# Single-row fetches by two DMA queues in a graph network on one Trainium2 core: byte offsets, loads of sixteen, higher rates and a third buffer

## The chip, the cores and the metric

The kernel runs on one core of a Trainium2 chip. The core has TensorE (PE, matrix products), VectorE (DVE), ScalarE (ACT), GpSimd (POOL) and SyncE (SP); each has its own instruction queue and works in the order of that queue, and the five meet at semaphores. DMAs are issued by SP, ACT and POOL and move data between DRAM and SBUF (128 partitions); PSUM holds the products. The metric is the device time of one execution in microseconds, smaller is better.

## The reference

The inputs are a graph of 12,500 nodes with 128 float32 features each and 212,500 edges, sorted by their target `dst`, with an `edge_weight` and a type from 0 to 7. Three layers follow each other (the file calls them layers 0, 1 and 2):

```python
edge_in = x[src] * edge_weight[:, None]                       # layer 0
msg = relu(edge_in @ W_msg + b_msg)
x1 = layernorm(x + relu(segment_sum(msg, dst) @ W_out + b_out))
xt = einsum('nd,rde->rne', h, W)                              # layers 1 and 2,
h = relu(segment_sum(xt[edge_type, src], dst) + h @ SW + b)   # from h = x1
out = layernorm(x1 + h)
```

Each layer gathers one row of 128 floats for every edge from a table in DRAM and adds the rows up by target. The tables are `msg_table` (12,500 rows, x times W_msg) and, for layers 1 and 2, `rel_table0` and `rel_table1` with one row for each node and type (100,352 rows).

## The kernel before

**Groups, tiles, steps.** The edges are cut into groups of eight tiles of 128 edges, 208 groups in layer 0 and 197 in each of layers 1 and 2. Two groups (16 tiles) make a step, so a layer has some 104 or 98 steps. In each step `fused_edges` handles two groups, and then `node_step` takes one block of 128 nodes, some steps behind the edges, through the layer's end (product, norm, next table). All five engines run through the same steps from lists written out by `fused_loop`; nothing is a loop on the chip.

**A group.** POOL gathers its tiles into `rows` (`static_gather`, L705, one indirect DMA for 128 rows), in a ring of eight groups: before it refills a slot it waits until PE has used it. DVE builds the one-hot matrices (L824) and in layer 0 scales every tile by its edge weights (L846); ACT applies relu in layer 0 (L673) or only passes the word on (L678); PE multiplies each tile with its one-hot matrix into PSUM (L872); DVE adds the result to `agg` (L859).

**The fetched tiles.** In some groups the eighth tile doesn't come from POOL. The class `Fetch` has it fetched row by row, by SP (`by_sync`, even groups) or by ACT (`by_act`, odd groups). `starts` and `rates` say from which step of each layer on, and how many rows a step: SP 24, 32 and 32, ACT 0, 24 and 24. So SP completes a tile in 5 1/3 steps in layer 0 and in 4 in the others, 17, 23 and 23 tiles; ACT makes 0, 17 and 17; in all 97 tiles, 12,416 rows. `Fetch.eight` does eight rows: it loads eight row numbers from the list `ids` in SBUF to registers (L801), and for each row computes the byte address in a register and starts a DMA of 512 bytes (L807). A tile is used two steps after its last row; it lies in one of `FETCHES` = 2 buffers of its queue, so that the first of its rows waits for the use of the tile before the last one (L795). The lists are made by DVE: for layer 0 a copy in `dve_layout`, for the others two instructions in `dve_trim`.

**Order on the queues.** SP's step is: the node work's DMAs (L1213 loads x, L1220 stores the table, L1226 stores the normed block), then its fetches. In layer 0 `sync_trim` puts more between them: for each of the two groups of a step a value load and a DMA to `kind_line` (L1584, L1586), with eight fetches behind each, then the DMA to `kind_of` (L1594), for which DVE waits before it picks each node's own row (L1140, L1147), and the last eight fetches. ACT's step is: the activations of the first group, eights number 0 and 2, those of the second group, eight number 1, then its node work, with the copy of the table from PSUM to SBUF (L1051) that DVE's second product (L1147) waits for. In layer 0 ACT fetches nothing.

Of the kernel before, what the change touches and what calls it, by code (L numbers as in the profile page):

```python
# [36 lines left out]
FETCHES = 2  # L37
EIGHT = 8
MOST = 80
# [60 lines left out]
def build(nc, x, src, dst, edge_type, edge_weight, W_msg, b_msg, W_out, b_out,  # L100
# [27 lines left out]
    with ctx:  # L128
# [6 lines left out]
        def ring_sems(name, n):  # L135
# [74 lines left out]
        extra = {"SP": spare_float[:, 2 * P:4 * P].rearrange("p (k d) -> p k d", k=2),  # L210
                 "ACT": spare_int[:, 4 * P:6 * P].bitcast(F32).rearrange("p (k d) -> p k d", k=2)}
# [160 lines left out]
        def dve_layout(sems, chunks, sorted_edges):  # L372
# [8 lines left out]
            for c in range(chunks):  # L381
# [8 lines left out]
                if not sorted_edges:  # L390
                    nc.vector.tensor_copy(ids[0][0:ROWS, c, :], e_src[:, GROUP - P:GROUP])
# [357 lines left out]
        class Fetch:  # L749


            def __init__(self, name, starts, rates, q):
                self.name = name
                self.starts = starts
                self.rates = rates
                self.groups = []
                self.base = []
# [16 lines left out]
            def tile(self, m):  # L774
                return extra[self.name][:, m % FETCHES, :]

            def wait(self, eng, m):

                eng.wait_ge(s_fetched[self.name][m % FETCHES], 16 * P * (m // FETCHES + 1))

            def eight(self, eng, layer, step, k):
# [7 lines left out]
                m, g = self.base[layer] + i, self.groups[layer][i]  # L789
                c, p = divmod(g, SIDE if layer else ROWS)  # L790
                if e == 0:
                    tables_ready(eng, layer)
                if part == 0:
                    if m >= FETCHES:
                        eng.wait_ge(edge_main.prod, self.uses[m - FETCHES] + 1)  # L795
                    if layer:
                        eng.wait_ge(s_stage, STAGES * c + PACKED)
                    else:
                        eng.wait_ge(lay.flag, 1)
                table = rel_tables[layer - 1] if layer else msg_table  # L800
                _, at = nc.values_load_multi_w_load_instructions(  # L801
                    ids[1 if layer else 0][p:p + 1, c, part * EIGHT:(part + 1) * EIGHT],
                    engines=[eng.engine], min_val=0, max_val=(NP * R if layer else N) - 1,
                    skip_runtime_bounds_check_because="the DMA checks its address")
                for j in range(EIGHT):
                    row = part * EIGHT + j
                    eng.dma_start(self.tile(m)[row:row + 1, :], table[bass.ds(at[j], 1), :]  # L807
                                  ).then_inc(s_fetched[self.name][m % FETCHES], 16)

        by_sync = Fetch("SP", (9, 1, 1), (24, 32, 32), 0)  # L810
        by_act = Fetch("ACT", (0, 1, 1), (0, 24, 24), 1)
# [623 lines left out]
        def dve_trim(step):  # L1435
# [27 lines left out]
            for c, beat in trim_beats(step):  # L1463
# [48 lines left out]
                else:  # L1512
                    closer(beat - BUILD_PACK - 1, 0)
                    if beat == BEATS - 1:
                        linked(v.tensor_scalar(held_int[0:r, 0:P], word[:, GROUP - P:GROUP],
                                               P.bit_length() - 1, None,
                                               ALU.logical_shift_right))
                        linked(v.tensor_scalar(ids[1][0:r, c, :], held_int[0:r, 0:P], -1.0, 0.0,
                                               ALU.add, ALU.max))
# [49 lines left out]
        def sync_trim(eng, step):  # L1569
# [27 lines left out]
            by_sync.eight(eng, 0, step, 2)  # L1597

        def fused_edges(eng, layer, step):
# [4 lines left out]
            for q in range(PAIR):  # L1604
# [22 lines left out]
                elif eng is nc.scalar:  # L1627
# [5 lines left out]
                    for k in range(q, by_act.rates[layer] // EIGHT, PAIR):  # L1633
# [204 lines left out]
```

## Time and profile before

| | |
|---|---|
| median of 3 runs | 8,691.48 us (8,671.66 to 8,698.19) |
| the profiled execution's own time | 8,760.86 us |
| its span | 8,759.1 us, 83,654 instructions |
| granted TensorE clock | 0.61 of full speed in the mean |
| PE busy | 2,867.2 us (33%) |
| weight loads (PEld) | 2,251.3 us (26%) |
| DVE busy | 2,703.9 us (31%) |
| ACT busy | 614.4 us (7%) |
| POOL busy | 4,471.7 us (51%) |
| DMA | 54 GB/s in the mean, 471 MB |
| rows fetched by SP | 2,176 from `msg_table`, 5,888 from the others |
| rows fetched by ACT | 4,352 |

The profile is of one execution; its times are a little over the median of the runs. Busy times leave out instructions that only handle registers, semaphores and branches, and those that issue DMAs; SP does nothing else, so it has no line there, and its queue (SPq) is to be read from the timeline, the chain and the views by line. A line such as L807 is that of the kernel's file. Layer 0 lasts from about 150 to 3,075 us, layer 1 from 3,137 to 5,855, layer 2 from 5,890 to the end.

### The profile page before, as it was taken

How to read it: one execution, taken by the hardware profiler on the slowest of the kernel's cores; microseconds unless marked ns; L12 is line 12 of the kernel's file. 1: busy time of each engine (PE TensorE's matmuls, PEld its weight loads, DVE VectorE, ACT ScalarE, POOL GpSimd, SP SyncE). 2: the span in 40 equal slices, each digit the busy share in tenths (PEclk: the TensorE clock that was granted, in tenths of full speed). 3: DMA queues.
4: the chain of work that ended last, by engine and by line, in shares of the span. 5: the costliest groups of instructions: out<-in, count | busy, mean ns of one | idle time of the engine just before them, and what ended most of it. 6: DMA issues, size and time to landing. Idle time of an engine off the chain costs nothing.

```text
span 8759.1 us, 83654 instructions
## 1 busy us (share of the span) xinstructions
PE 2867.2 (33%) x11892; PEld 2251.3 (26%) x11892; DVE 2703.9 (31%) x5898; ACT 614.4 (7%) x1351; POOL 4471.7 (51%) x4738
## 2 busy tenths in 40 slices
PE   5233333333333324333333333341222222222222
PEld 4222222222222213222222222221222222222222
DVE  3864655555444522222222222230111111111111
ACT  2111111111111100000000000000000000000000
POOL 5645445455555445555555555545555445455544
PEclk7666666666666656666666666665555555555556
DMA  4112122212222112111121111111111111111111
GB/s 127 45 57 63 56 59 59 59 57 61 59 62 60 57 52 60 56 55 56 58 59 58 57 58 58 57 58 43 41 43 41 39 39 41 41 41 41 43 39 37
DMA packets 287776, 471.48 MB, mean 54 GB/s; under 512 B 113324, under 2 KB 178644, under 8 KB 287204
## 3 DMA queue, kind: packets, MB, share of 16 engines
q0 software_dynamic: 151008, 309.57, 13.6%
q1 hardware_dynamic: 126340, 153.80, 5.1%
q14 instruction: 476, 3.90, 0.1%
q10 hardware_dynamic: 9856, 2.64, 0.1%
q8 instruction: 96, 1.57, 0.1%
HBM read 343.56 MB, written 122.05 MB: 53 GB/s over the span
## 4 chain that ended last, share of the span: by engine, by line
SPq 52%; issue 36%; DVE 4%; PE 3%; DMA 2%; another core or an unknown queue 2%; ACTq 2%; ACT 0%; POOL 0%; DVEq 0%; POOLq 0%
SPq L807 40%; SPq L801 7%; SPq L1584 2%; PE bank L872 2%; ACTq L807 1%; DMA kind_line<-weight 1%; SPq L1586 1%; SPq L1226 1%; SPq L1213 1%; DVE rows L846 1%; SPq L1220 1%; PE bank L1108 0%; DVE picked L1147 0%; DVE onehot L824 0%
## 5 line engine op out<-in xcount | busy, mean ns | idle before, releaser
L705 POOL DMA_INDIRECT rows<-rel_table,rel_index x3072 | 2905.6, 946 | 2819.8 <-PE bank L872 1277.7
L872 PE MATMUL bank<-onehot,rows 128*128 128x128 f32 x9438 | 1846.4, 374 | 3626.5 <-ACTq L678 1980.2
L872 PEld LDWEIGHTS bank<-onehot,rows 128*128 128x128 f32 x9438 | 1739.8, 281 | 3863.5 <-ACTq L678 2018.7
L705 POOL DMA_INDIRECT rows<-msg_table,msg_index x1583 | 1497.6, 946 | 1419.5 <-PE bank L872 837.4
L859 DVE TENSOR_TENSOR agg<-agg,bank 128x128 f32 x602 | 171.7, 285 | 3599.9 <-PE bank L872 2119.5
L1108 PE MATMUL bank<-wr,feat 128*128 128x512 f32 x784 | 691.2, 1035 | 570.5 <-ACT feat L1067 329.3
L824 DVE TENSOR_TENSOR onehot<-bank,place 128x1024 f32<-128x1024 f32 x602 | 732.2, 1216 | 17.1 <-ACT agg L1037 3.8
L1147 DVE TENSOR_TENSOR picked<-bank,chosen 128x512 f32<-128x512 f32 x392 | 261.4, 689 | 1128.3 <-ACT tab L1051 849.3
L1094 PE MATMUL bank<-wo,sums 128*128 128x128 f32 x196 | 74.5, 481 | 1291.8 <-issue 735.9
L1108 PEld LDWEIGHTS bank<-wr,feat 128*128 128x128 f32 x784 | 229.2, 322 | 795.8 <-issue 444.3
L846 DVE SCALAR_TENSOR_TENSOR rows<-rows,weight,bank 128x128 f32<-128x128 f32 x1583 | 424.9, 341 | 0.0
L1094 PEld LDWEIGHTS bank<-wo,sums 128*128 128x128 f32 x196 | 46.9, 297 | 1313.5 <-issue 749.2
L1158 DVE TENSOR_REDUCE place<-picked 128x128 f32<-128x1024 f32 x196 | 371.3, 1894 | 9.9
L1140 DVE TENSOR_SCALAR chosen<-columns,kind_of 128x8 f32<-128x8 f32 x196 | 48.3, 247 | 990.9 <-DMA kind_of<-kind_line 770.4
L673 ACT ACTIVATE rows<-rows 128x512 f32<-128x512 f32 (+1 forms) x416 | 258.9, 624 | 1054.8 <-DVE rows L846 810.1
L1071 ACT ACTIVATE sums<-agg 128x128 f32<-128x128 f32 x196 | 60.6, 309 | 2926.5 <-DVE agg L859 1189.0
L1051 ACT ACTIVATE tab<-bank 128x512 f32<-128x512 f32 x196 | 115.8, 591 | 2008.8 <-issue 1652.7
L1168 DVE COPY tab<-bank 128x512 f32<-128x512 f32 x196 | 134.1, 684 | 14.1 <-PE bank L1108 12.8
L1097 PE MATMUL bank<-ident,sums 128*128 128x128 f32 x98 | 42.2, 431 | 275.9 <-ACT sums L1071 160.4
L1060 ACT ACTIVATE feat<-bank 128x128 f32<-128x128 f32 x98 | 27.1, 277 | 1155.0 <-DVE picked L1147 844.4
L1097 PEld LDWEIGHTS bank<-ident,sums 128*128 128x128 f32 x98 | 16.7, 170 | 301.1 <-ACT sums L1071 177.6
L1122 PEld LDWEIGHTS bank<-ident,place 128*128 128x128 f32 x392 | 78.6, 278 | 51.9 <-issue 45.8
(133 smaller groups left out, 1455.8 us busy)
## 6 DMA issues: line engine op xcount, KB each, us to landing
rel_table<-tab SPq DMA_DIRECT2D x196, 512.0 KB, 2.6
weight<-rel_table SPq DMA_DIRECT2D x5888, 0.5 KB
rel_index<-rel_table ACTq DMA_DIRECT2D x4352, 0.5 KB
rows<-rel_table,rel_index POOLq DMA_INDIRECT x3072
weight<-msg_table SPq DMA_DIRECT2D x2176, 0.5 KB
rows<-msg_table,msg_index POOLq DMA_INDIRECT x1583
x_dram<-normed SPq DMA_DIRECT2D x98, 64.0 KB
xin<-x_dram SPq DMA_DIRECT2D x98, 64.0 KB, 1.8
```

What stands on the lines that cost most here:

```text
L673: nc.scalar.activation(v, v, ACT.Relu).then_inc(sems.ready, 1)
L705: nc.gpsimd.indirect_dma_start(rows[:, u, t, :], None, table, bass.IndirectOffsetOnAxis(ap=table_index[:, g, t:t + 1], axis=0)).then_inc(e ...
L801: _, at = nc.values_load_multi_w_load_instructions(ids[1 if layer else 0][p:p + 1, c, part * EIGHT:(part + 1) * EIGHT], engines=[eng.engin ...
L807: eng.dma_start(self.tile(m)[row:row + 1, :], table[bass.ds(at[j], 1), :]).then_inc(s_fetched[self.name][m % FETCHES], 16)
L824: nc.vector.tensor_tensor(out=onehot[:, k, :, :], in0=ps_columns.unsqueeze(1).to_broadcast([P, TPG, P]), in1=group_cols(spots, st, lead).r ...
L846: ins = nc.vector.scalar_tensor_tensor(out=tile, in0=product if convert else tile, scalar=w[:, 0, t:t + 1], in1=bm[:, :] if convert else p ...
L859: nc.vector.tensor_tensor(out=window, in0=window, in1=ps_edge[k][:, 0:P], op=ALU.add).then_inc(sems.added, 1)
L872: ins = nc.tensor.matmul(ps_edge[k][:, 0:P], tile, onehot[:, k, t, :], start=t == 0, stop=t == TPG - 1)
L1108: ins = nc.tensor.matmul(ps_tab[h][:, :], feat[:, st.u, :], wr[layer][:, h * H:(h + 1) * H], start=True, stop=True)
L1147: v.tensor_tensor(out=picked[:, h * H:(h + 1) * H].rearrange("p (r e) -> p r e", r=R // 2), in0=ps_tab[h][:, :].rearrange("p (r e) -> p r ...
L1158: nc.vector.tensor_reduce(out=own_row_of(st.b), in_=picked[:, :].rearrange("p (r e) -> p e r", r=R), axis=AX, op=ALU.add).then_inc(sems.pi ...
L1584: base = eng.value_load(base2[0:1, g:g + 1], min_val=0, max_val=N)
```

## The change

The lists `ids` hold byte offsets (row number times 512) in place of row numbers. A fetch reads the table as bytes at the offset that the register holds. Offsets are loaded sixteen at a time, and each sixteen one ahead of its use, into two sets of registers. Each queue has three buffers instead of two (one more tile, `third`, for each). The rates become 32, 40 and 40 rows a step for SP and 24, 32 and 32 for ACT, which now takes part in layer 0 from step 9 on. By the rule of `Fetch.__init__` these are 23, 29 and 29 tiles for SP and 17, 23 and 23 for ACT: 144 tiles, 18,432 rows. ACT's eights of a step are split evenly, the first half after the first group and the second after the second.

```diff
-FETCHES = 2
+FETCHES = 3
+LOAD = 16
+ROW_BYTES = 4 * P
+BYTE = mybir.dt.uint8
...
                 if not sorted_edges:
-                    nc.vector.tensor_copy(ids[0][0:ROWS, c, :], e_src[:, GROUP - P:GROUP])
+                    nc.vector.tensor_scalar(ids[0][0:ROWS, c, :], e_src[:, GROUP - P:GROUP],
+                                            float(ROW_BYTES), None, ALU.mult)
...
+            def load(self, eng, layer, e):
+                i, part = divmod(e, P // LOAD)
+                if i >= len(self.groups[layer]):
+                    return
+                c, p = divmod(self.groups[layer][i], SIDE if layer else ROWS)
+                if part == 0:
+                    if layer:
+                        eng.wait_ge(s_stage, STAGES * c + PACKED)
+                    else:
+                        eng.wait_ge(lay.flag, 1)
+                _, self.at[e % 2] = nc.values_load_multi_w_load_instructions(
+                    ids[1 if layer else 0][p:p + 1, c, part * LOAD:(part + 1) * LOAD],
+                    engines=[eng.engine], min_val=0,
+                    max_val=((NP * R if layer else N) - 1) * ROW_BYTES,
+                    skip_runtime_bounds_check_because="the DMA checks its address")
...
-                _, at = nc.values_load_multi_w_load_instructions(
-                    ids[1 if layer else 0][p:p + 1, c, part * EIGHT:(part + 1) * EIGHT],
...
+                    self.load(eng, layer, 0)
+                if part == 0 and m >= FETCHES:
+                    eng.wait_ge(edge_main.prod, self.uses[m - FETCHES] + 1)
+                n, half = divmod(e, LOAD // EIGHT)
+                if half == 0:
+                    self.load(eng, layer, n + 1)
+                table = (rel_tables[layer - 1] if layer else msg_table).rearrange(
+                    "n d -> (n d)").bitcast(BYTE)
                 for j in range(EIGHT):
                     row = part * EIGHT + j
-                    eng.dma_start(self.tile(m)[row:row + 1, :], table[bass.ds(at[j], 1), :]
+                    at = self.at[n % 2][half * EIGHT + j]
+                    eng.dma_start(self.tile(m)[row:row + 1, :].bitcast(BYTE),
+                                  table[bass.ds(at, ROW_BYTES)].rearrange("(p n) -> p n", p=1)
                                   ).then_inc(s_fetched[self.name][m % FETCHES], 16)
 
-        by_sync = Fetch("SP", (9, 1, 1), (24, 32, 32), 0)
-        by_act = Fetch("ACT", (0, 1, 1), (0, 24, 24), 1)
+        by_sync = Fetch("SP", (9, 1, 1), (32, 40, 40), 0)
+        by_act = Fetch("ACT", (9, 1, 1), (24, 32, 32), 1)
...
-                                               P.bit_length() - 1, None,
-                                               ALU.logical_shift_right))
-                        linked(v.tensor_scalar(ids[1][0:r, c, :], held_int[0:r, 0:P], -1.0, 0.0,
-                                               ALU.add, ALU.max))
+                                               P.bit_length() - 1, ROW_BYTES.bit_length() - 1,
+                                               ALU.logical_shift_right,
+                                               ALU.logical_shift_left))
+                        linked(v.tensor_scalar(ids[1][0:r, c, :], held_int[0:r, 0:P],
+                                               -float(ROW_BYTES), 0.0, ALU.add, ALU.max))
...
-            by_sync.eight(eng, 0, step, 2)
+            for k in range(PAIR, by_sync.rates[0] // EIGHT):
+                by_sync.eight(eng, 0, step, k)
...
-                    for k in range(q, by_act.rates[layer] // EIGHT, PAIR):
+                    eights = by_act.rates[layer] // EIGHT
+                    for k in range(q * eights // PAIR, (q + 1) * eights // PAIR):
                         by_act.eight(eng, layer, step, k)
```

## Rows read from the trace of the kernel before

**Rows 1.** The chain of waits of the page: shares by engine, then by line

```profile
SPq 52%; issue 36%; DVE 4%; PE 3%; DMA 2%; another core or an unknown queue 2%; ACTq 2%; ACT 0%; POOL 0%; DVEq 0%; POOLq 0%
SPq L807 40%; SPq L801 7%; SPq L1584 2%; PE bank L872 2%; ACTq L807 1%; DMA kind_line<-weight 1%; SPq L1586 1%; SPq L1226 1%; SPq L1213 1%; DVE rows L846 1%; SPq L1220 1%; PE bank L1108 0%; DVE picked L1147 0%; DVE onehot L824 0%
```

**Rows 2.** Waits of SP's queue, layer 1 (3360 to 5815): total, times, longest

```profile
SPq L1220 <- DVE tab L1168: 1.2, 3, 0.4
```

**Rows 3.** Timeline of all engines, end of an SP tile: start and length, us

```profile
7041.05 0.95 POOL L705 DMA_INDIRECT rows<-rel_table,rel_index  x1 [0.30 <-issue]
7041.15 17.50 SPq L807 DMA_DIRECT2D weight<-rel_table  x32
7042.30 0.94 POOL L705 DMA_INDIRECT rows<-rel_table,rel_index  x1 [0.30 <-issue]
...
7059.67 1.65 PE L872 MATMUL bank<-onehot,rows 128*128 128x128 f32 x6 [23.90 <-ACTq L678]
...
7062.56 0.95 POOL L705 DMA_INDIRECT rows<-rel_table,rel_index  x1 [19.31 <-PE bank L872]
```

**Rows 4.** SP's fetch DMAs, layers 0, 1, 2: ns min/median/max, first and last start

```profile
L807 SPq DMA_DIRECT2D weight<-msg_table x2176: 1/228/1424, 391.8 to 3027.7; - x198
...
L807 SPq DMA_DIRECT2D weight<-rel_table x2816: 1/228/1412, 3359.9 to 5814.1; - x188
...
L807 SPq DMA_DIRECT2D weight<-rel_table x2816: 1/228/1407, 6103.3 to 8721.0; - x188
```

**Rows 5.** Gathers of POOL, layer 1: duration ns, first and last start

```profile
L705 POOL DMA_INDIRECT rows<-rel_table,rel_index x1524: 942/947/962, 3136.5 to 5827.0; - x191
```

**Rows 6.** SP's fetches (ns min/median/max) and loads (chain), 7046 to 7058, POOL idle

```profile
L807 SPq DMA_DIRECT2D weight<-rel_table x23: 227/228/263, 7046.0 to 7057.6; - x23
L807 SPq FUSED_REGOPS  x23: 37/37/37, 7047.1 to 7057.9; - x23
L807 SPq MOVE weight<-rel_table x23: 29/29/38, 7047.1 to 7057.9; - x23
...
7046.23 0.79 SPq L801
...
7054.53 0.80 SPq L801
```

**Rows 7.** SP in 1850 to 1868, POOL gathering: timeline, then MOVEs (ns)

```profile
1852.10 11.96 SPq L807 DMA_DIRECT2D weight<-msg_table  x4
1864.76 0.71 SPq L1213 DMA_DIRECT2D xin<-in_x_dram  x1
1866.17 0.00 SPq L1220 DMA_DIRECT2D rel_table<-tab  x1
...
L807 SPq MOVE weight<-msg_table x2: 699/1042/1385, 1857.8 to 1862.0; - x2
```

**Rows 8.** SP's queue in layer 0, one step without gathers: timeline

```profile
2009.06 0.36 SPq L1213 DMA_DIRECT2D xin<-in_x_dram  x1
...
2013.19 3.21 SPq L807 DMA_DIRECT2D weight<-msg_table  x8
...
2018.66 3.15 SPq L807 DMA_DIRECT2D weight<-msg_table  x8
2021.91 0.36 SPq L1594 DMA_DIRECT2D kind_of<-kind_line  x1
```

**Rows 9.** Loads of one value from SBUF on SP, layer 0: duration ns

```profile
L1584 SPq TENSOR_LOAD <-msg_index x181: 2/530/1220, 395.1 to 3022.6; - x181
```

**Rows 10.** Waits of DVE, layer 0 (1500 to 3050): total us, times, longest

```profile
DVE chosen L1140 <- DMA kind_of<-kind_line: 470.4, 38, 24.4
```

**Rows 11.** The page's costliest groups: busy us, mean ns, idle us before

```profile
L824 DVE TENSOR_TENSOR onehot<-bank,place 128x1024 f32<-128x1024 f32 x602 | 732.2, 1216 | 17.1 <-ACT agg L1037 3.8
L1147 DVE TENSOR_TENSOR picked<-bank,chosen 128x512 f32<-128x512 f32 x392 | 261.4, 689 | 1128.3 <-ACT tab L1051 849.3
L846 DVE SCALAR_TENSOR_TENSOR rows<-rows,weight,bank 128x128 f32<-128x128 f32 x1583 | 424.9, 341 | 0.0
```

More of the change, by code:

```diff
@@ L209, in build @@
         spare_float = weight[:, GROUPS:, :].rearrange("p g t -> p (g t)")
-        extra = {"SP": spare_float[:, 2 * P:4 * P].rearrange("p (k d) -> p k d", k=2),
-                 "ACT": spare_int[:, 4 * P:6 * P].bitcast(F32).rearrange("p (k d) -> p k d", k=2)}
+        third = sb("third", [P, 2, P])
+        extra = {"SP": [spare_float[:, 2 * P:3 * P], spare_float[:, 3 * P:4 * P],
+                        third[:, 0, :]],
+                 "ACT": [spare_int[:, 4 * P:5 * P].bitcast(F32),
+                         spare_int[:, 5 * P:6 * P].bitcast(F32), third[:, 1, :]]}
         low = sb("low", [ROWS, CHUNKS])
@@ L756, in __init__ @@
                 self.groups = []
+                self.at = [None, None]
                 self.base = []
@@ L774, in tile @@
             def tile(self, m):
-                return extra[self.name][:, m % FETCHES, :]
+                return extra[self.name][m % FETCHES]
             def wait(self, eng, m):
                 eng.wait_ge(s_fetched[self.name][m % FETCHES], 16 * P * (m // FETCHES + 1))
+            def load(self, eng, layer, e):
[13 more added lines that the diff above has]
+                    skip_runtime_bounds_check_because="the DMA checks its address")
             def eight(self, eng, layer, step, k):
@@ L788, in eight @@
                     return
-                m, g = self.base[layer] + i, self.groups[layer][i]
-                c, p = divmod(g, SIDE if layer else ROWS)
+                m = self.base[layer] + i
                 if e == 0:
                     tables_ready(eng, layer)
[L793 to L800, printed above, removed]
-                _, at = nc.values_load_multi_w_load_instructions(
-                    ids[1 if layer else 0][p:p + 1, c, part * EIGHT:(part + 1) * EIGHT],
-                    engines=[eng.engine], min_val=0, max_val=(NP * R if layer else N) - 1,
-                    skip_runtime_bounds_check_because="the DMA checks its address")
+                    self.load(eng, layer, 0)
[6 more added lines that the diff above has]
+                    "n d -> (n d)").bitcast(BYTE)
                 for j in range(EIGHT):
                     row = part * EIGHT + j
-                    eng.dma_start(self.tile(m)[row:row + 1, :], table[bass.ds(at[j], 1), :]
+                    at = self.at[n % 2][half * EIGHT + j]
+                    eng.dma_start(self.tile(m)[row:row + 1, :].bitcast(BYTE),
+                                  table[bass.ds(at, ROW_BYTES)].rearrange("(p n) -> p n", p=1)
                                   ).then_inc(s_fetched[self.name][m % FETCHES], 16)
-        by_sync = Fetch("SP", (9, 1, 1), (24, 32, 32), 0)
-        by_act = Fetch("ACT", (0, 1, 1), (0, 24, 24), 1)
+        by_sync = Fetch("SP", (9, 1, 1), (32, 40, 40), 0)
+        by_act = Fetch("ACT", (9, 1, 1), (24, 32, 32), 1)
         def fetched_by(layer, st):
```

## The prediction

> **What bounds the kernel now.** The chain of waits comes first: SP's queue and "issue" hold 88% of it, and nearly all of the queue's share is line 807, the single-row fetches, and line 801, their loads [rows 1]. PE, DVE, ACT and POOL are busy for at most half of the span, so the question is whether SP is late or only present. SP's own waits answer it: in 2,455 us of layer 1 it waits 1.2 us [rows 2]. The timeline shows what hangs on it: SP's last fetch of a tile ends at 7058.65, PE, idle for 23.90 us, goes on at 7059.67, and POOL, idle for 19.31 us behind PE, at 7062.56 [rows 3]. So in layers 1 and 2 the time is SP's time for a tile of 128 rows; POOL has room.
>
> The pace: 2,816 fetches take 2,454 us in layer 1, 0.872 us each, and 2,618 us in layer 2, 0.930 us each [rows 4]. At 32 a step that is 27.9 and 29.8 us a step. In layer 0 it is 2,636 us for 2,176, 1.212 us each, or 29.1 us for the 24 of a step [rows 4]; there DVE waits for kind_of, which SP sends, 470 us in 1,550 [rows 10]. SP paces all three layers.
>
> A fetch has two speeds. Where POOL gathers nothing, it is FUSED_REGOPS 37 ns, MOVE 29, DMA 228 and gaps; sixteen with their two loads take 7054.53 - 7046.23 = 8.30 us, 0.519 each, of which a load of eight is 0.80 to 0.83 and a fetch alone 0.41 [rows 6]. Where POOL gathers, everything SP issues is slow: four fetches in 11.96 us, a MOVE of 700 to 1,385 ns in place of 29 [rows 7]. **It matters whether this delay belongs to the DMA or to the instruction.** In the same stretch the two DMAs of lines 1213 and 1220, with one wait between them and no arithmetic, start 1.41 us apart, where a fetch's three instructions need 3 to 4 us [rows 7]. I read it as a delay for each instruction. That step decides my sign.
>
> **The change, part by part.** (1) Arithmetic: one of three instructions goes. Without gathers a FUSED_REGOPS costs 37 ns and its gap, 0.07 in all, so 0.41 becomes 0.34. (2) Loads: one for 16 rows instead of 8. Its length hardly depends on the count: one value takes 530 ns at the median [rows 9], eight 790 to 800 [rows 6]. Bounds for sixteen: 0.8 us and, if it is two of eight, 1.65. I take 0.83, since one to eight added little; a fetch then costs 0.34 + 0.05 = 0.39, in 2.06 instructions where it had 3.125. Issued one sixteen ahead, a load could hide altogether; I count nothing for it, as SP stands in it now. (3) Rates: SP 24/32/32 rows a step becomes 32/40/40, ACT 0/24/24 becomes 24/32/32: 47 tiles or 6,016 fetches more. (4) POOL issues 47 gathers fewer; their pitch is 1.25 us [rows 3, 5], and with idle time behind PE they are worth nothing by themselves, but they shorten the slow stretches a little. (5) A third buffer relaxes a wait on PE that costs SP nothing now [rows 2]: zero, and covered by SP being late. (6) On DVE the two changed instructions for the lists run a few times in all, and no instruction is added: zero beside DVE's idle time. (7) Waits: ACT's fetches of layer 0 begin with waits for the message table and the lists, which POOL and SP used long before step 9; queued behind them would be ACT's activations, at no cost, since they are over.
>
> **Layer 1.** Of a step of 27.9 us POOL gathers 15.56 tiles at 1.25 = 19.5 us; the other 8.4 us hold, at 0.519 and 0.015 for the table's store, 15.8 fetches. So 16.2 fall into the 19.5 us: 1.20 each, a delay of 0.67 for some 3.2 instructions, 0.21 each. After: gathers 15.44 tiles, 19.3 us; a fetch in them 0.40 + 2.1 x 0.21 = 0.84, makes 22.9; the other 17.1 at 0.40 need 6.9 us. Step **26.2 us, 1.7 less**.
>
> **Layer 2.** Two more DMAs a step make the undelayed fetch 0.547; 10.3 us outside the gathers hold 18.7, and 13.3 fall into 19.5 us: 1.47, a delay of 0.29 an instruction. After: 0.414 + 2.1 x 0.29 = 1.02 in 19.3 us makes 18.9; 21.1 at 0.414 need 8.7. Step **28.0, 1.75 less**.
>
> **Layer 0.** SP does other work too: from 2009.06 to 2022.27 it takes 13.2 us for 16 fetches (8.3), so 4.9 us, in 18 instructions [rows 8]. A step is 12.5 + 4.9 = 17.4 us without delays. Outside 19.8 us of gathers 9.3 are done, so 8.1, holding 43 of its 93 instructions, share 11.7 us of delay: 0.27 each. After: 32 x 0.39 + 4.9 = 17.4 again, with 84 instructions, 4.8 for each us: in 19.45 us of gathers 19.45 / (1 + 4.8 x 0.27) = 8.5 get done, 8.9 remain, 28.4 us. But ACT now issues 24 fetches in this layer. Whether that deepens the delay no row shows; below, nothing (layer 1, with ACT fetching, has 0.21, less than layer 0), above, by the spread between layers, 0.08. I take 0.06, nearer the top as ACT's load is new: 29.4 us, **0.3 more**, and 0.4 with ACT's own queue (below).
>
> Sum: layers 1 and 2 have 92 such steps each: 1.7 x 92 + 1.75 x 92 = 317 us less; layer 0, 95 steps from step 9: 40 us more. Net -277 on the profiled execution's 8,760.9, which is 0.8% above the median of the runs; on 8,691.5 that gives **8,415 us, -3.2%**. About 0.3%, 26 us, is what a measurement of this kernel can tell from no change.
>
> **Rivals.** (B) *The delay goes with the DMA.* Then the arithmetic saves nothing where POOL gathers. Layer 1: 0.65 for each DMA, 18.2 fetches in 19.3 us, 21.8 outside take 8.8: 28.1, +0.2. Layer 2: 29.9, +0.15. Layer 0: 38 DMAs where 30 were, 0.84 each: 30.0, +0.9. Sum +117, more with ACT's in layer 0: **8,810, slower**. For it: a MOVE may only show a stall that an earlier DMA began. Against it: the bare DMAs of line 1213 and 1220 above. It decides once some seven tenths of the delay go with the DMA. The Trainium skill ("Perfetto Trace Analysis", section on the HWDGE DMA instruction) speaks for it: the descriptor generator is shared by the two issuing sequencers and locked for one at a time, and the lock wait counts in the DMA's own duration. By that the delay would stand in the DMAs; the trace has it in the MOVEs as well, so it disagrees or shows it late.
>
> (C) *ACT becomes the pace of layer 0.* ACT issues 12 fetches after each group's activations, before it copies the table for which DVE waits, and DVE then works for ACT's next group. DVE waits for kind_of 8.6 us a step by rows 10 (470 of 1,550 us, 55 steps) and some 12 with what is put down to no releaser, so this loop is some 17 us long now. 24 fetches of ACT add 24 f, of which DVE's second group (1.2 + 8 x 0.34) and half its product (0.7) [rows 11], with small things some 6 us, run beside: 11 + 24 f. At f = 0.75, my price of an ACT fetch with its share of delays, 29 us, level with SP; at 0.95 it is 34, 4.9 x 95 = 465 us, and the total 8,691 - 317 + 465 = **8,840**. It decides from f = 0.77 on.
>
> (D) *SP gets quick enough to meet the next bound.* Fewer instructions on two queues could also shrink each one's delay. At three quarters of it, layer 1 comes to 0.40 + 0.33 = 0.73 a fetch in the gathers and 25.1 us, layer 2 to 27.0: 2.8 x 184 = 515 us less, **8,220**. At half of it they come to 23 and 25 us, just above the 19.3 us of gathers, and SP begins to wait.
>
> (E) *It doesn't do what it says*: sixteen values come as two loads (0.05 a fetch more, 1.6 to 2 us a step, 8,930), or the byte form of the DMA takes the 0.36 us of line 1213's [rows 8] and not 0.23: 4 to 5 us a step, **9,700**.
>
> **How the numbers follow.** Forecast 0.45, B 0.20, C 0.15, D 0.14, E 0.06. Faster: forecast and D, with a third of C (f between 0.77 and 0.85 leaves a gain): 0.62. Slower: B, E, most of C: 0.30. Within 0.3%: 0.08. The range runs from 8,130, a little below D's 8,220, to 8,860, just above B and C; it leaves out E and the far ends of C and D.
>
> **What would show it.** Right: no FUSED_REGOPS in the fetches; undelayed fetches 0.34 us apart; half as many loads for each row, still 0.8 us; during gathers two delays a fetch, not three; steps of 26 and 28 us in layers 1 and 2, SP still without waits, and PE going on right after its last fetch. Layer 0 near 29 us. Wrong: delayed fetches as far apart as before (B); DVE in layer 0 waiting for ACT's table copy (C); SP waiting for PE's products and POOL without idle time (D); loads in pairs or DMAs of 0.36 us (E).

## The result, and the profile after

The changed kernel takes **8,894.06 us** (median of 4 runs, 8,877.40 to 8,910.21), the kernel before, beside it, 8,687.79 (8,671.66 to 8,698.19): ratio 1.0239, 95% interval 1.0213 to 1.0265. The forecast was 8,415 us; the change makes the kernel slower, and the time lies just above the top of the range. The profiled execution took 8,910.21 us, its span is 8,908.4 us with 82,756 instructions, the granted clock 0.611.

One thing has to be known to read what follows: the same kernel meets two conditions. In some groups of runs made together, among them those of this result and of the trace of before, SP's and ACT's instructions come in pieces of about 0.70 us beside POOL's gathers, and the kernel before has medians of 8,662 to 8,784 us; in others they don't, and its medians are 6,007 to 6,021. I call the two *with* and *without the delay*. What decides between them is open. It isn't the kernel, and the number of the chip doesn't tell it either: the record has chip 9 without the delay in the seventh group below and with it in the eighth, four minutes later (whether the same number is the same chip each time, it doesn't say). Every ratio below is against the kernel before, run beside it.

The page of the changed kernel, chain of waits by engine and by line:

```profile
SPq 47%; issue 36%; ACTq 5%; DVE 3%; PE 3%; DMA 2%; another core or an unknown queue 2%; ACT 0%; POOL 0%; DVEq 0%; POOLq 0%
SPq L829 36%; SPq L801 6%; ACTq L829 4%; PE bank L895 2%; SPq L1608 2%; DMA kind_line<-weight 1%; SPq L1610 1%; DMA kind_of<-kind_line 1%; SPq L1249 1%; ACTq L801 1%; PE bank L1131 1%; SPq L1243 1%; DVE picked L1170 1%; SPq L1236 1%
```

It is the chain of [rows 1]: SP's fetches (now L829), their loads (L801) and issue. ACT's fetches have grown from 1% to 4%. Waits of SP's queue in layer 1, as in [rows 2] (3320 to 6100):

```profile
SPq L1241 <- ACT tab L1074: 26.1, 5, 8.1
SPq L1243 <- DVE tab L1191: 1.9, 8, 0.4
```

SP still waits for nothing that counts, 28 of 2,780 us. The end of an SP tile in the timeline, as in [rows 3]:

```profile
4519.01 5.48 SPq L829 DMA_DIRECT2D weight<-rel_table  x16
4525.55 1.65 PE L895 MATMUL bank<-onehot,rows 128*128 128x128 f32 x6 [13.98 <-ACTq L685]
4526.99 0.64 PE L895 MATMUL bank<-onehot,weight 128*128 128x128 f32 x2
...
4528.44 0.94 POOL L712 DMA_INDIRECT rows<-rel_table,rel_index  x1 [19.14 <-PE bank L895]
```

SP's last fetch ends at 4524.49, PE goes on at 4525.55 and POOL, after 19.14 us behind PE, at 4528.44. SP sets the pace as before. The fetches are shorter, though. Pieces of the chain between 7020 and 7024, POOL idle, which answer to [rows 6]:

```profile
7021.24 1.28 SPq L801
7022.62 0.26 SPq L829
7022.98 0.23 SPq L829
7023.31 0.23 SPq L829
7023.63 0.23 SPq L829
7023.95 0.23 SPq L829
```

A fetch follows the last one after 0.32 to 0.33 us (0.41 before, 0.34 forecast), and no FUSED_REGOPS is left. But one load of sixteen takes 1.28 us, not 0.83, and SP stands in it: 0.08 a fetch instead of 0.05, 0.40 in all. Where the time is, us a step, first counted as the forecast counts, by SP's fetches (in layers 1 and 2 from the second tile on), then by the starts of DVE's add of each group (L859 before, L882 after):

| | before | forecast | after |
|---|---|---|---|
| layer 0, by SP's fetches | 29.1 | 29.4 | 30.8 |
| layer 1, by SP's fetches | 27.9 | 26.2 | 28.5 |
| layer 2, by SP's fetches | 29.8 | 28.0 | 28.7 |
| layer 0, DVE's adds while SP fetches | 29.2 | | 31.0 |
| layer 0, DVE's adds, all steps | 28.25 | | 29.99 |
| layer 1, DVE's adds, all steps | 27.7 | | 28.4 |
| layer 2, DVE's adds, all steps | 29.2 | | 28.25 |

Layer 0 lasts 180 us longer, layer 1 64 longer, layer 2 90 less. Steps below are by DVE's adds. The two profiles differ by 149 us and the medians of the runs by 206, since the profiled execution of before was above its own median; in which layer the other 57 us lie is not known. In layer 0, DVE's waits from 1500 to 3250 answer to [rows 10]:

```profile
DVE chosen L1163 <- DMA kind_of<-kind_line: 664.8, 42, 27.1
DVE chosen L1163 <- issue: 84.4, 9, 13.8
...
DVE picked L1170 <- ACT tab L1074: 24.6, 7, 7.0
```

DVE waits for `kind_of`, which SP sends, 665 us in 1,750 (470 in 1,550 before), and for ACT's table copy 25. So here, with the delay, layer 0 is late by SP, not by the loop of rival C.

### The profile page after: what moved, and what is told of

It reads as the page before. It is cut to its first block, busy times and chain, and to the rows that moved or that the text cites. A ratio compares the mean times of both kernels' runs of the same rounds, so it can differ in the third digit from the quotient of the medians.

```text
span 8908.4 us, 82756 instructions
## 1 busy us (share of the span) xinstructions
PE 2899.2 (33%) x11892; PEld 2261.1 (25%) x11892; DVE 2706.0 (30%) x5898; ACT 619.3 (7%) x1374; POOL 4415.9 (50%) x4691
## 4 chain that ended last, share of the span: by engine, by line
SPq 47%; issue 36%; ACTq 5%; DVE 3%; PE 3%; DMA 2%; another core or an unknown queue 2%; ACT 0%; POOL 0%; DVEq 0%; POOLq 0%
SPq L829 36%; SPq L801 6%; ACTq L829 4%; PE bank L895 2%; SPq L1608 2%; DMA kind_line<-weight 1%; SPq L1610 1%; DMA kind_of<-kind_line 1%; SPq L1249 1%; ACTq L801 1%; PE bank L1131 1%; SPq L1243 1%; DVE picked L1170 1%; SPq L1236 1%
## 5 line engine op out<-in xcount | busy, mean ns | idle before, releaser
L712 POOL DMA_INDIRECT rows<-rel_table,rel_index x3048 | 2875.3, 943 | 2793.1 <-PE bank L895 1318.0
L712 POOL DMA_INDIRECT rows<-msg_table,msg_index x1560 | 1472.4, 944 | 1622.7 <-PE bank L895 1033.3
L882 DVE TENSOR_TENSOR agg<-agg,bank 128x128 f32 x602 | 171.3, 284 | 3255.2 <-PE bank L895 1713.7
L1191 DVE COPY tab<-bank 128x512 f32<-128x512 f32 x196 | 133.9, 683 | 14.2 <-PE bank L1131 13.0
L1203 DVE TENSOR_SCALAR normed<-y,mv,rstd 128x128 f32<-128x128 f32 x196 | 70.4, 359 | 67.9 <-ACT feat L1083 35.7
L1060 ACT ACTIVATE agg<-bank,br 128x512 f32<-128x512 f32 (+1 forms) x50 | 33.9, 678 | 781.7 <-DMA rows<-rel_table,rel_index 379.6
```

The source lines that it names most:

```text
L712: nc.gpsimd.indirect_dma_start(rows[:, u, t, :], None, table, bass.IndirectOffsetOnAxis(ap=table_index[:, g, t:t + 1], axis=0)).then_inc(e ...
L882: nc.vector.tensor_tensor(out=window, in0=window, in1=ps_edge[k][:, 0:P], op=ALU.add).then_inc(sems.added, 1)
```

## The experiments

The theories. I: the delay beside gathers is a price for each instruction, as the prediction read it. B: for each DMA. C: ACT's fetches lengthen the loop DVE, ACT, DVE in layer 0. From the third group on S, too, read from the two traces: SP loses a fixed share of the gathers' time, 11.3 us a step, whatever it issues, since undelayed work plus 11.3 gives 28.4, 28.8 and 28.7 us for layers 1, 2 and 0 of before (27.9, 29.8 and 29.1 measured) and 28.1 and 28.5 for layers 1 and 2 of after.

**First: which part costs?** (1) The changed kernel with the rates of before:

```diff
-        by_sync = Fetch("SP", (9, 1, 1), (32, 40, 40), 0)
-        by_act = Fetch("ACT", (9, 1, 1), (24, 32, 32), 1)
+        by_sync = Fetch("SP", (9, 1, 1), (24, 32, 32), 0)
+        by_act = Fetch("ACT", (9, 1, 1), (0, 24, 24), 1)
```

> The changed kernel with the rates of before (SP 24, 32, 32; ACT 0, 24, 24; 97 tiles): arithmetic, load of sixteen and third buffer alone. If the delay beside the gathers goes with each instruction (theory I), a fetch loses a third of it and its undelayed time falls from 0.52 to 0.41 us: steps of 25.7, 23.4 and 25.1 us in the three layers, 7,500 us in all. If it goes with each DMA (theory B), steps of 27.2, 25.3 and 26.9 us, 8,000 us. If SP is not what paces, 8,690.

(2) The kernel before with the new rates alone, `(32, 40, 40)` and `(24, 32, 32)` from step 9, two buffers and the arithmetic kept:

> The kernel before with the rates of after (SP 32, 40, 40; ACT 24, 32, 32; 144 tiles, two buffers, with the register arithmetic and loads of eight). SP as the pace, with each instruction delayed: 32 to 34 us a step in all layers, 9,800 us. If POOL's 47 gathers fewer are worth more than the fetches cost: under 8,690.

(3) The changed kernel without ACT in layer 0:

```diff
-        by_act = Fetch("ACT", (9, 1, 1), (24, 32, 32), 1)
+        by_act = Fetch("ACT", (9, 1, 1), (0, 32, 32), 1)
```

> The changed kernel with ACT's rate in layer 0 back at 0 (SP 32, 40, 40; ACT 0, 32, 32). If ACT's fetches are what makes layer 0 longer (31 us a step against 29 before), its step goes to 28.4 us and the whole to 8,650. If SP's own 32 rows a step do it, the step stays at 30.5 to 31 us and the whole at 8,850 or more.

(4) The changed kernel with all rates 0, so that POOL gathers every tile:

> The changed kernel with all rates 0: POOL gathers all 16 tiles of a step, SP and ACT fetch no row. If SP paces the kernel in its fetches, the step falls to POOL's 16 x 1.25 = 20 us or to what comes next (ACT and DVE in layer 0, about 20 too): 6,300 to 7,000 us. If the fetches earn what they cost, 8,700 us or more.

Measured: before 6,007.46 us; (1) 6,008.24, ratio 1.0001 (0.9991 to 1.0011); (2) 6,802.36, 1.132 (1.1301 to 1.1339); (3) 5,970.34, 0.9936 (0.9919 to 0.9953); (4) 6,128.96, 1.02 (1.0183 to 1.0217). The expectations in absolute times missed, by 20 to 31% for (1) to (3) and by 3% for (4): these runs were without the delay. SP's fetches in layers 1 and 2 without the delay, here of the changed kernel as it is (ns, min/median/max):

```profile
L829 SPq MOVE weight<-rel_table x3840: 29/29/38, 3207.6 to 6044.4; - x192
L829 SPq DMA_DIRECT2D weight<-rel_table x3840: 227/228/597, 3207.6 to 6044.4; - x192
```

and in the trace of the result (layer 1):

```profile
L829 SPq MOVE weight<-rel_table x2432: 2/29/1407, 3514.0 to 6070.4; - x188
L829 SPq DMA_DIRECT2D weight<-rel_table x2432: 2/228/1412, 3514.1 to 6070.5; - x188
```

The medians are the same; the maxima are 38 and 597 ns there, 1,407 and 1,412 here. Without the delay POOL paces: its 15.5 gathers a step at 1.25 us are 19.4 us, and layers 1 and 2 take 19.3 to 19.5 a step in (1) and (3). So each tile that is fetched is worth one gather: (3) fetches 127 tiles, 30 more than before, 6,007 - 30 x 1.25 = 5,970, as measured. The missing arithmetic, the load of sixteen and the third buffer are worth nothing by themselves there (1). At the new rates the arithmetic matters again: (2) takes 21.3 to 21.5 us a step in layers 1 and 2 and 23.4 in layer 0.

**Second: the change itself, without the delay.**

> The changed kernel, unchanged. In the four runs before this one the kernel before took 6,007 us and not 8,688. If the delay beside the gathers is a condition of the chip on which a program runs, and this chip has none: steps of POOL's pace, 15.44 tiles x 1.25 = 19.3 us in layers 1 and 2, and 5,940 to 5,980 us beside 6,007, ratio 0.99 to 0.995; with the delay 8,890 beside 8,690, ratio 1.02. If SP's and ACT's rates cost by themselves, slower than before on either.

6,199.85 us against 6,011.46, ratio 1.0313 (1.0296 to 1.033). Slower here as well, and all of it in layer 0: 21.35 us a step against 19.2 in (3), up to 25.1 in its first steps with fetches, and 19.3 from step 70 on; layers 1 and 2 take 19.33 in both. DVE's waits in layer 0 (300 to 2150) of the change:

```profile
DVE picked L1170 <- ACT tab L1074: 422.8, 83, 7.0
DVE chosen L1163 <- DMA kind_of<-kind_line: 73.6, 52, 3.0
```

with POOL's wait for the buffers that the loop holds back,

```profile
POOL rows L712 <- PE bank L895: 227.4, 51, 14.8
```

and of (3), without ACT's fetches there, DVE's and then POOL's:

```profile
DVE rows L869 <- DMA rows<-msg_table,msg_index: 247.1, 100, 5.3
DVE chosen L1163 <- DMA kind_of<-kind_line: 69.5, 27, 5.7
...
DVE picked L1170 <- ACT tab L1074: 2.8, 2, 1.4
...
POOL rows L712 <- PE bank L895: 1.5, 5, 0.3
```

423 us of waits for ACT's table copy against 3: that is rival C's loop, DVE to ACT to DVE, at its place. Without ACT's fetches it is DVE that waits for POOL's gathers (247 us); with them POOL, the pace otherwise, stands 227 us, which is the loss. It costs only while DVE also makes the lists of the next layers; those steps end near step 70.

**Third: how much of ACT, when, and is SP's rate part of it?** ACT at 16 rows a step in layer 0, `(16, 32, 32)`:

> The changed kernel with ACT at 16 rows a step in layer 0 instead of 24. Without the delay, in steps 9 to 72, in which DVE also trims, layer 0 takes 23.5 us a step with ACT at 24 rows and 19.3 at 0. If the loop DVE to ACT to DVE (11 + 24 f, f = 0.41 us) sets it, 8 rows less give 3.3 us back: 20.2 us and 6,000 us in all. If the fetches of both queues disturb each other instead, less than 1.5 us of it: 6,100 or more. Beside a kernel before of 8,690 us: between 8,700 and 8,890.

ACT at 24, but from step 74 of layer 0 on:

```diff
-        by_act = Fetch("ACT", (9, 1, 1), (24, 32, 32), 1)
+        by_act = Fetch("ACT", (74, 1, 1), (24, 32, 32), 1)
```

> The changed kernel with ACT's fetches of layer 0 beginning at step 74, after DVE's last trimming beat, instead of 9. Loop theory: the loop is shorter there by DVE's trimming work and stays below POOL's 19.4 us, so nothing is lost and ACT's 5 tiles of layer 0 gain 1.25 us each: 5,960 to 5,970 us. If ACT's fetches cost in every step of layer 0: 6,030 or more. Beside a kernel before of 8,690 us: 8,700 to 8,850.

SP back at 24 in layer 0, ACT as in the change:

> The changed kernel with SP at 24 rows a step in layer 0 instead of 32, ACT at 24. Without the delay SP has time left and nothing changes in the loop: 6,200 us and 6 tiles x 1.25 more, 6,205. Beside a kernel before of 8,690 us, where SP paces: 8 rows less are 3.3 us of undelayed work a step, 8,894 less up to 300, 8,600 to 8,700; if ACT's fetches set layer 0 there too, 8,890.

Before 6,007.16 us; 16 rows 5,978.79, 0.9951 (0.9932 to 0.9971); from step 74 5,962.81, 0.993 (0.9907 to 0.9952); SP at 24 6,187.24, 1.03 (1.027 to 1.033). Layer 0: 19.2, 19.1 and 21.3 us a step. SP's rate is free here, ACT's 24 rows are the whole loss. With the undelayed price of a fetch, 0.40, rival C's own formula gives 11 + 16 x 0.40 = 17.4 us and 11 + 24 x 0.40 = 20.6; while DVE makes lists (steps 10 to 69) 19.9 and 23.3 are measured. The eight rows cost the 3.3 us that the formula says, its constant is some 2.6 too low.

**Fourth: the load of sixteen alone.** ACT from step 74 again, with `LOAD = 8`, beside which only the ACT start differs from the change:

> As the run with ACT from step 74 (5,963 us beside 6,007), but eight offsets a load. A load of sixteen takes 1.27 us and one of eight took 0.80, so a row costs 0.10 instead of 0.08 us: 40 rows 0.8 us more a step on SP, which has some 2 us to spare beside POOL's 19.3: 5,960 to 5,975 us. If SP has no such room, 6,050 or more. Beside a kernel before of 8,690 us, where SP paces: 1 to 2 us a step more than the same with sixteen.

8,732.63 us against 8,661.75, 1.0085 (1.0066 to 1.0105): these runs had the delay. Eights load in about 0.80 us, so a fetch costs 0.42 instead of 0.40. Layer 0 takes 29.4 us a step while only SP fetches (steps 9 to 73) and 31.9 and 32.3 in the last stretches of ten, where ACT fetches too. In the kernel before, where ACT fetches nothing in layer 0, the same last stretches are no longer than the others (28.4 and 28.9). In the change, with ACT throughout, it is 31.0. ACT's 24 rows cost some 2 to 3 us a step with the delay as well, here within one execution, and not by the loop: DVE waits 1.7 us for ACT's table copy in these last stretches, and 389 for `kind_of`. Layers 1 and 2 take 27.9.

**Fifth: repeats.** Three kernels were run again, to see them with the delay, and met the condition without it.

> The changed kernel at the rates of before (97 tiles), on a chip where the kernel before takes about 8,690 us. Theory S (the delay is a fixed time a step, some 11.3 us of the 19.4 us of gathers, whatever SP issues): a step is SP's undelayed work plus 11.3: layers 1 and 2, 32 x 0.41 + 0.5 + 11.3 = 24.8 us (27.9 and 29.8 before), layer 0, 24 x 0.41 + 4.9 + 11.3 = 26 (29.1 before): 8,690 - 290 - 460 - 290 = 7,650 us. Theory I (delay for each instruction): 7,500. Theory B (for each DMA): 8,000. SP not the pace: 8,690. On a chip without the delay: 6,008.

> All rates 0, on a chip where the kernel before takes about 8,690 us. If only SP and ACT are delayed and POOL's pitch stays 1.25 us: layers 1 and 2 at 20 us a step, layer 0 at 20 to 22: 6,100 to 6,500 us, far under both kernels. If the gathers themselves are slow there, over 8,000. On a chip without the delay: 6,129.

> The changed kernel with ACT at 0 in layer 0, on a chip where the kernel before takes about 8,690 us. By theory S for SP alone: layer 0 at 32 x 0.41 + 4.9 + 11.3 = 29.3 us a step where the changed kernel has 31.2: 8,894 - 1.9 x 95 = 8,710 us. If ACT's fetches don't matter there: 8,890. On a chip without the delay: 5,970.

Before 6,018.56; 6,018.94 (1.0002), 6,138.16 (1.02) and 5,983.47 (0.9941, 0.9922 to 0.9961). They repeat the first results.

**Sixth: fewer rows.** SP `(16, 16, 16)`, ACT `(0, 16, 16)`, 55 tiles, and the old rates beside it:

> The changed kernel at 16 rows a step for SP in all layers and 16 for ACT in layers 1 and 2 (55 tiles). On a chip without the delay POOL paces: 6,129 (no fetches) less 55 x 1.25 = 6,060 us. Where the kernel before takes about 8,690: by theory S (delay fixed at 11.3 us a step) SP needs 18.4 us in layers 1 and 2 and 22.8 in layer 0, so POOL's 19.7 sets two layers: 6,400 us. By theory I or B nearly the same, so this run says whether SP's queue alone makes the slow condition slow: if it stays above 7,500, POOL's gathers or ACT are slow there as well.

> The changed kernel at the rates of before (97 tiles). Where the kernel before takes about 8,690 us: theory S (delay fixed for each step) 7,650 us, steps of 26, 24.8 and 25 us; theory I (for each instruction) 7,500; theory B (for each DMA) 8,000; SP not the pace, 8,690. Without the delay: 6,008, as measured twice.

Before 6,007.60; 6,058.73 (1.0084, 1.0064 to 1.0103) and 6,007.56 (1.0000). With 55 tiles 6,129 - 55 x 1.25 = 6,060: the price of 1.25 us a tile holds downward too.

**Seventh: two buffers, and more rows for ACT.** Old rates with `FETCHES = 2`; then SP `(24, 32, 32)` with ACT `(74, 1, 1), (24, 40, 40)`:

> The changed kernel with the rates of before (SP 24, 32, 32 rows a step, ACT 0, 24, 24) and with two buffers in place of three: what is left of the change is the missing arithmetic and the load of sixteen. Where the fetches are not delayed beside POOL's gathers, every theory says 6,008 us, as with three buffers, since POOL paces. Where they are delayed the theories part. S (SP loses a fixed 11.3 us or so of every step, a share of the time of the gathers): steps of 17.4 less 24 x 0.10 = 15.0, plus 11.3 = 26.3 us in layer 0, 17.1 less 32 x 0.10 = 13.9, plus 11.3 = 25.2 in layer 1, 25.6 in layer 2: 7,650 us. I (delay for each instruction): 7,500 us. B (delay for each DMA): only the 0.10 us a fetch in undelayed stretches is won, 8,000 to 8,300 us.

> The changed kernel with the rates of SP of before (24, 32, 32) and ACT at 24 from step 74 of layer 0, then 40, 40: SP fetches 63 tiles, ACT the rest, about 126 tiles in all. Where the fetches are not delayed, POOL paces and each tile fetched is worth its gather's 1.25 us: 6,129 - 126 x 1.25 = 5,971 us. Where they are delayed: S as in the kernel with two buffers, with ACT's fetches in the last 30 steps of layer 0 adding 2 us a step, 7,700 us if ACT's 40 fetches a step stay beside SP's, 8,000 if ACT with 40 x 0.66 = 26.4 us a step and its own activations becomes the pace of layers 1 and 2.

Before 6,021.42; 6,022.39 (1.0002, 0.9993 to 1.0012) and 6,168.39 (1.0244, 1.0227 to 1.0262). The third buffer is worth nothing without the delay. The second result was a miss, 5,971 being expected: at 40 rows ACT's loop catches layer 1, 21.25 us a step for 19.4, while layer 0, where ACT fetches late, and layer 2, where no table is copied, take 19.2 and 19.4. DVE's waits in layer 1 (2200 to 4200):

```profile
DVE picked L1170 <- ACT tab L1074: 1123.5, 91, 14.4
DVE agg L882 <- PE bank L895: 234.5, 91, 12.7
```

The wait alone doesn't show the loss: in the last kernel below, with ACT at 32 rows, it is 902 us (2200 to 4000) at 19.4 us a step. POOL's wait for PE does, 195 us here and 6 there.

**Eighth: the parts without the rates, with the delay.** The kernel of (1) once more:

> The changed kernel at the rates of before once more (three buffers), for the chip condition in which fetches are delayed. Without the delay 6,008 us or so on any chip, all theories. With it: S (a fixed loss of 11.3 us a step) 7,650 us, I (for each instruction) 7,500, B (for each DMA) 8,000 to 8,300.

These runs had the delay: 8,388.07 us against 8,784.30, ratio 0.9535 (0.9462 to 0.9609), from two runs against three. So without arithmetic, with loads of sixteen and three buffers at the old rates the kernel gains 4.7% where the delay is, and the change as made loses 2.4%: **the new rates cost it some 7% there** (1.0239 / 0.9535 = 1.074, from two groups of runs). By the two traces 467 of some 530 us of this lie in layer 0, 20 in layer 1 and 45 in layer 2. In layer 0 both rates count: 26.1 us a step at the old rates (steps 10 to 79), 29.4 with SP at 32 rows and ACT still silent (load of eight), 31.0 in the change. But it isn't the time of any theory, and its steps say why: 25.5 us in layer 0, where S said 26.3, but 28.2 and 27.8 in layers 1 and 2, where S said 25.2 and 25.6. SP waits for nothing there either (3100 to 5500, all its waits):

```profile
SPq L1243 <- DVE tab L1191: 0.4, 1, 0.4
```

SP spends 28 us on 32 fetches where the change spends 28 us on 40. What differs is how POOL gathers. The kernel before, layer 1, the first gather of each of three groups:

```profile
4048.18 0.95 POOL L705 DMA_INDIRECT rows<-rel_table,rel_index  x1 [2.62 <-PE bank L872]
...
4059.20 0.95 POOL L705 DMA_INDIRECT rows<-rel_table,rel_index  x1 [2.58 <-PE bank L872]
...
4071.54 0.94 POOL L705 DMA_INDIRECT rows<-rel_table,rel_index  x1 [2.64 <-remote]
```

The changed kernel at the old rates, layer 1, with sixteen gathers between the two pauses:

```profile
3895.80 0.94 POOL L712 DMA_INDIRECT rows<-rel_table,rel_index  x1 [4.00 <-remote]
3897.06 0.94 POOL L712 DMA_INDIRECT rows<-rel_table,rel_index  x1 [0.31 <-issue]
...
3919.76 0.94 POOL L712 DMA_INDIRECT rows<-rel_table,rel_index  x1 [4.29 <-remote]
```

Before, POOL rests at least 2.6 us after every seven or eight gathers; now it rests after fifteen or sixteen. And SP gets slower the longer POOL goes on. One run of sixteen gathers of the change, POOL from 3930.94 to 3950.60, SP's chain:

```profile
3930.34 0.23 SPq L829
3930.66 0.23 SPq L829
...
3940.90 0.70 SPq L829
3941.62 0.71 SPq L829
...
3947.23 1.40 SPq L829
...
3952.83 0.70 SPq L829
3953.63 0.23 SPq L829
3953.86 0.04 issue
3953.89 1.25 SPq L801
```

SP's DMAs start 0.32 us apart up to 3932, then, to name some, at 3939.5, 3941.6 and 3943.0, at last at 3947.2, 3950.0 and 3952.8, 2.8 us apart, and from 3953.6 on, some 3 us after POOL's last gather, undelayed again. So I call a row of gathers a run as long as no two start over 2.2 us apart, take it up to 2.55 us after its last start (the pitch of 1.25 and 1.3 more), and count all of SP's DMAs in it, from the traces' starts, over the middle of layers 1 and 2 and in layer 0 from SP's first fetches on:

| us for each DMA of SP | runs of 8 | runs of 16 |
|---|---|---|
| before, layer 1 | 1.03 (156 runs) | one run |
| before, layer 2 | 0.96 (96) | 1.68 (32) |
| change, layer 1 | 0.74 (71) | 1.16 (41) |
| change, layer 2 | 0.71 (76) | 1.12 (48) |
| change at old rates, layer 1 | none | 1.23 (84) |
| change at old rates, layer 2 | few | 1.18 (82) |
| before, layer 0 (no ACT) | few | 1.21 (86) |
| change, layer 0 (with ACT) | few | 1.27 (84) |
| change at old rates, layer 0 (no ACT) | none | 0.98 (89) |
| load of 8, layer 0 up to step 73 (no ACT) | none | 0.91 (62) |
| load of 8, layer 0 from step 74 on (with ACT) | few | 1.27 (25) |

What falls and what stays open: the delay is this time less the undelayed one, 0.52, 0.55 and 0.58 for each DMA in layers 1, 2 and 0 of before, 0.41, 0.41 and 0.48 after.

| runs | delay before | after | factor |
|---|---|---|---|
| of 8, layer 1 | 0.51 | 0.33 | 0.65 |
| of 8, layer 2 | 0.41 | 0.30 | 0.73 |
| of 16, layer 2 | 1.13 | 0.71 | 0.63 |
| of 16, layer 0, ACT silent (change at old rates) | 0.63 | 0.50 | 0.79 |

B, a delay for each DMA, wants a factor of 1 and falls. S, one fixed loss of 11.3 us in every step, falls too: it said 25.2 us for layer 1 at the old rates and 28.2 are measured. "For each instruction" wants 0.66 (2.07 instructions a fetch for 3.13), and two of the four factors fit it. But a loss that depends on the length of the run alone, whatever SP issues in it, wants 0.75 to 0.83 (undelayed time after by before), and the other two lie there or near: a run loses 5.5 us before and 4.9 after, 4.7 and 4.6, 14.2 and 13.1, 11.0 and 10.7, in the order of the table. The runs don't decide between these two, and neither says why a run of 16 costs less in layer 0 with ACT silent than in layer 2.

**Last: the candidate for both.** SP at 24 in layer 0, ACT from step 74, layers 1 and 2 as changed:

```diff
-        by_sync = Fetch("SP", (9, 1, 1), (32, 40, 40), 0)
-        by_act = Fetch("ACT", (9, 1, 1), (24, 32, 32), 1)
+        by_sync = Fetch("SP", (9, 1, 1), (24, 40, 40), 0)
+        by_act = Fetch("ACT", (74, 1, 1), (24, 32, 32), 1)
```

> The changed kernel with SP at 24 rows a step in layer 0, as before the change, and ACT's fetches of layer 0 from step 74 on; layers 1 and 2 at the changed rates. Without the delay beside gathers POOL paces: about 129 tiles of fetched rows, 6,129 - 129 x 1.25 = 5,968 us, ratio 0.993. With it: layer 0 as in the kernel at the old rates (25.5 us a step, 2 us more over its last 30 steps), layers 1 and 2 as measured with either rates, 28.2 us: 8,400 to 8,450 us, ratio 0.96 to 0.97. If ACT's fetches of layer 0 were what costs rather than SP's rate there, this comes out no faster than the change with ACT late (29.0 us a step in layer 0, 8,700 us).

5,983.91 us against 6,020.08, ratio 0.994 (0.9923 to 0.9956), without the delay. It is faster than both there, if by little (0.6% against the kernel before, as ACT from step 74 alone with 0.7%); with the delay it was not measured, and the 8,400 us stay an expectation.

## Why the prediction was wrong, point by point

In short, two sizes failed. The delay of layer 1 was carried over as a constant, but it grows along POOL's runs of gathers, and these got longer; and ACT's effect on SP's delay in layer 0 was taken at 0.06 us an instruction, where some 0.17 is measured within one execution. The first is worked out from traces and not shown by a run of its own.

**What bounds the kernel** was read rightly, and held after the change: SP without waits, PE going on a microsecond after its last fetch.

**(1) The arithmetic, (2) the load.** 0.32 to 0.33 us a fetch for the 0.34 said. The load of sixteen was taken at 0.83 because one value takes 530 ns and eight 800; it takes 1.27 (median without the delay), between the bounds 0.8 and 1.65: 0.53, 0.80, 1.27 are some 0.04 to 0.06 for each further value. In the sum a fetch is 0.40 for 0.39: up to 0.4 us a step, some 100 us over the three layers. The Trainium skill ("DMA: Bandwidth & Descriptors", section "Latency and other measured facts", the row on tensor_load) gives about 600 ns as a floor; the trace has 530 for one value.

**The delay belongs to the instruction**, the step said to decide the sign, was half borne out: at equal length of POOL's runs the delay of a DMA fell to 0.63 to 0.79 of itself as the third instruction went, so it doesn't go with the DMA; whether it goes with the instruction or with the run is not decided. The Trainium skill ("Perfetto Trace Analysis", section on the HWDGE DMA instruction) places such a wait in the DMA's own duration; the traces with the delay have pieces of 0.70 us in MOVEs as well, so the measurement goes against the DMA alone. Yet the sign was wrong, by what stands around this step.

**Layer 1, forecast 26.2, is 28.5 by SP's fetches and 28.4 by DVE's adds.** The step that failed is "16.2 fall into the 19.5 us: 1.20 each, a delay of 0.67 for some 3.2 instructions, 0.21 each", carried over to the new kernel as a constant of its 19.3 us of gathers. The delay is no constant: it grows along an unbroken run of gathers. Layer 1 of before had runs of eight, all but one. Had they stayed, 2.0 runs of 11.0 us would have taken 29.7 DMAs, and the 11 others of the step's 41 at 0.41 need 4.6 us: 26.6, the forecast nearly. It has 0.91 runs of eight and 0.53 of sixteen: 21.0 us with 23.1 DMAs, and 17.9 x 0.41 = 7.3: 28.3, as measured. That is bookkeeping from the traces, with the runs of before put in for the first sum; no run held their length fixed.

**Layer 2, forecast 28.0, is 28.7 by SP's fetches**: of the 1.75 us of gain 1.1 came, and of the missing 0.65 the load's price is up to 0.4. Before, it already had both kinds of runs.

Why the runs grew isn't shown by a run of its own. The diff has a candidate that the prediction passed over: ACT's eights are no longer dealt out 2 and 1 around the second group's word to PE but evenly, at the old rates 1 and 2. With eight fetches between the two groups (change at the old rates) all runs are of sixteen, with sixteen between them (before) hardly any in layer 1. But layer 2 of before and the change, with sixteen too, have both kinds, so this is not all of it, and the third buffer is not excluded. Nor is it explained that layers 1 and 2 come to 27.7 to 29.2 us in all four kernels measured with the delay, at 32 and at 40 rows a step, with loads of eight and of sixteen.

**Layer 0, forecast 29.4, is 30.8 by SP's fetches and 31.0 by DVE's adds.** The step that failed is the size of "whether that deepens the delay no row shows; below, nothing, above, by the spread between layers, 0.08. I take 0.06". In runs of sixteen of one execution (load of 8) a DMA of SP takes 0.91 us while ACT fetches nothing and 1.27 when it does, 0.36 or some 0.17 an instruction: outside both ends. In some 20.8 us of a step's run that is 22.9 DMAs or 16.4, and the 6.5 missing ones at the undelayed 0.47 are 3.1 us, where the steps grew by 2.7. Without ACT the forecast's step was 28.4, and 29.4 is measured there with loads of eight, whose fetch of 0.42 for the 0.39 of the forecast is 32 x 0.03 = 1.0 us a step: that part of the forecast stood. The change with ACT silent in layer 0 was never measured with the delay. Where the prediction compared layers 0 and 1 to bound it, the comparison was of runs of sixteen without ACT with runs of eight with it.

**The sum.** Forecast: -277 us. Measured between the two profiles: +149, of which by layer +180, +64 and -90, where +40, -156 and -161 were said. Layer 0 missed by 140, layer 1 by 220, layer 2 by 71, in part the load.

**The rivals.** Three totals lie near 8,894, E's 8,930 for loads in pairs, C's 8,840 and B's 8,810, and none by its mechanism. C's played hardly any part in the result (25 us of waits for the table copy in 1,750), but it is the whole of the loss without the delay, and its formula has the price of ACT's rows right. E fell, with one load and DMAs of 0.23 us, though the load costs 0.03 a fetch more than the forecast's where two loads were to cost 0.05. D fell with the delay; without it, SP is indeed quick enough and POOL is the next bound. What the prediction did not consider is that the profile might show one of two conditions only.

## What to carry to other kernels

A delay read from a stretch is a value at that stretch's conditions: tabulate it by how long its cause has been acting before multiplying it by a time, since an edit that moves other work can change that length. A cheaper operation and a higher rate are two changes: by itself the first was worth 4.7% here with the delay and nothing without it, and the second turned it into a loss in both. A queue that takes on fetches also carries a copy that another engine waits for; price the loop through it, at the time when the other engines of the loop are busiest.

## What the runs showed of the hardware

- This kernel meets two conditions, 8,662 to 8,784 us and 6,007 to 6,021 with the same program; what sets them is open. In the slower one instructions of SP and ACT that take 29 or 228 ns otherwise take 0.70 us and its multiples, nearly all of them while POOL issues indirect gathers, from 1.4 to 4.2 us into a run on (medians by layer), and up to some 3 us after its end. POOL's own pitch is 1.25 us in both. SP recovers 10.1, 11.4, 21.3 and 22.7 us after the first of 7, 8, 15 and 16 gathers (medians of the change's layer 1; within 0.1 us in the other layers and kernels counted, 1 and 2 of before, 2 of the change, 1 at the old rates), as if each gather took 1.42 us to be worked off where it takes 1.25 to issue; that is a reading of these times and was not tested.
- A load of values from SBUF to registers takes 0.53 us for one, 0.80 for eight and 1.27 for sixteen, and its queue stands in it, also when the values are needed only later. Loading one sixteen ahead hides none of it.
- Without register arithmetic single-row DMAs of one queue follow each other every 0.322 us; with it, every 0.41.
